# Operands of the last stage made from columns of x with factors by one-hot matmuls, in place of gathered rows that are multiplied and transposed

## The reference, cut to what matters

```
def _ln(x, g, b):
    m = jnp.mean(x, axis=-1, keepdims=True)
    v = jnp.mean((x - m) ** 2, axis=-1, keepdims=True)
    return (x - m) * jax.lax.rsqrt(v + EPS) * g + b
h = _ln(x, pw_g[pathway_ids], pw_b[pathway_ids])
h = _ln(h, cp_g[compartment_ids], cp_b[compartment_ids])
t = _ln(x, tm_g[time_steps], tm_b[time_steps])
s = _ln(x, ms_g[scale_type], ms_b[scale_type])
cat = jnp.concatenate([w[0]*h, w[1]*t, w[2]*m, w[3]*n, w[4]*r, w[5]*s], axis=-1)
u = _ln(silu(cat @ int_W1 + int_b1) @ int_W2 + int_b2, int_g, int_be)
q = clip(round(u / u_scale))      # by rows, to 255 levels
out = x + (q @ q_rhs) * u_scale * rhs_scale
```

## Time and profile before

| | us |
|---|---|
| median of 3 runs (lowest to highest) | 1751.22 (1750.68 to 1754.04) |
| the profiled execution | 1750.74 |
| its span | 1748.8 |
| PE busy | 1733.7 (99%) |
| DVE busy | 1192.6 (68%) |
| ACT busy | 878.1 (50%) |
| POOL busy | 786.8 (45%) |

### The profile page before, as it was taken

One profiled execution on the slowest core, in us unless ns is written; L12 is line 12 of the kernel. 1 busy time (PEld: TensorE's weight loads), 2 busy tenths in 40 slices (PEclk: granted clock), 3 DMA queues, 4 the chain that ended last, 5 costly groups with the idle time before them and its releaser, 6 DMA issues. The chain is left out here.

```text
span 1748.8 us, 23364 instructions
## 1 busy us (share of the span) xinstructions
PE 1733.7 (99%) x7935; PEld 1407.0 (80%) x7935; DVE 1192.6 (68%) x1756; ACT 878.1 (50%) x1301; POOL 786.8 (45%) x702
## 2 busy tenths in 40 slices
PE   9999999999999999999999999999999999999998
PEld 7888888888778888888888888778877787787786
DVE  8756667669989678786563335357886687587555
ACT  7655555565666565674562223243453443443433
POOL 1112221122766566665560000025577877878742
PEclk9999999999999999999999999999999999999999
DMA  6011110120233324222536568877645445544511
GB/s 208 1 49 49 48 39 9 49 73 25 97 132 119 134 97 168 97 97 85 187 139 222 193 197 281 325 254 245 217 132 183 143 159 175 155 159 152 170 38 61
DMA packets 121991, 234.36 MB, mean 134 GB/s; under 512 B 25618, under 2 KB 25874, under 8 KB 121892
## 3 DMA queue, kind: packets, MB, share of 16 engines
q1 hardware_dynamic: 91732, 157.63, 27.0%
q0 software_dynamic: 11776, 41.95, 7.0%
q10 hardware_dynamic: 18384, 33.56, 5.8%
HBM read 170.71 MB, written 58.72 MB: 131 GB/s over the span
## 5 line engine op out<-in xcount | busy, mean ns | idle before, releaser
L1070 PE MATMUL bank<-h_parts,mlp_w 128*128 128x512 f32 x2016 | 460.0, 389 | 4.6 <-DVE mlp_w L1493 3.3
L1070 PEld LDWEIGHTS bank<-h_parts,mlp_w 128*128 128x128 f32 x2016 | 378.0, 188 | 85.4 <-DVE mlp_w L1493 3.7
L353 PE MATMUL bank<-h_parts,gate_w 128*128 128x512 f32 x1536 | 351.1, 389 | 0.6 <-DVE h_parts L688 0.5
L353 PEld LDWEIGHTS bank<-h_parts,gate_w 128*128 128x128 f32 x1536 | 288.1, 188 | 61.9 <-issue 0.9
L2066 PE MATMUL bank<-operand_parts,int_w 128*128 128x512 f32 x1152 | 279.8, 396 | 0.5 <-DVE u_tiles L2716 0.4
L1135 PE MATMUL bank<-p_parts,mlp_out_w 128*128 128x512 f32 x1152 | 271.2, 393 | 0.0
L1135 PEld LDWEIGHTS bank<-p_parts,mlp_out_w 128*128 128x128 f32 x1152 | 213.8, 188 | 48.4 <-issue 4.2
L2066 PEld LDWEIGHTS bank<-operand_parts,int_w 128*128 128x128 f32 x1152 | 212.2, 188 | 47.1 <-issue 2.2
L615 POOL TENSOR_TENSOR decay_sq<-decay 128x512 f32<-128x512 f32 x32 | 39.3, 1227 | 278.8 <-DVE decay L701 278.8
L1408 POOL TENSOR_TENSOR product_out<-product_out,gelu 128x512 f32<-128x512 f32 x69 | 120.0, 1762 | 97.1 <-DVE product_out L1564 96.6
L1288 ACT ACTIVATE product_copy<-bank,vec_sb 128x512 f32<-128x512 f32 x144 | 99.1, 688 | 112.4 <-PE bank L1070 111.4
(11 more groups left out here) (311 smaller groups left out, 2760.4 us busy)
## 6 DMA issues: line engine op xcount, KB each, us to landing
p_tile<-p_d ACTq DMA_DIRECT2D x96, 256.0 KB, 4.8
p_d<-product_out SPq DMA_DIRECT2D x92, 256.0 KB, 2.0
raw_mlp_w<-mlp_gate_g SPq DMA_DIRECT2D x21, 512.0 KB, 3.7
raw_mlp_w<-mlp_fc_g SPq DMA_DIRECT2D x21, 512.0 KB, 4.4
xin<-xT SPq DMA_DIRECT2D x8, 1024.0 KB
hs_d<-u SPq DMA_DIRECT2D x8, 1024.0 KB, 5.0
hs_pair<-hs_d SPq DMA_DIRECT2D x8, 1024.0 KB, 7.5
x_columns<-xT SPq DMA_DIRECT2D x8, 1024.0 KB, 6.9
```

What stands on the lines that cost most here:

```text
L353: i = pe.matmul(bank[:], gw[:, w, s, k, m * P:(m + 1) * P], hr[:, q, t, k, :], start=k == 0 and n == 0, stop=k == KT - 1 and n == 2)
L1070: i = pe.matmul(bank[:], wb[g % 2][:, s, w, kk, :], hop[u % 2][o][:, t, kk, :], start=first and kk == 0 and n == 0, stop=kk == 1 and n == ...
```

## The change

**Time and scale operands.** x columns are normalised as columns. POOL makes, for each of the four column tiles k, two passes over 128x512 (`xhat_columns`): xn[k] = x column times 1/std, then plus shift, both along the tokens. The factors come from `spread`: SP stores `rstd` and `shift` to DRAM (`store_stats`; 16 bytes, the four tiles' values, a partition), and loads them back to all 128 partitions (`load_stats`, two loads of 2 KB a partition). In that row the tokens of one tile of 128 are 16 bytes apart, so `spread_of` reads it with a step of 16 bytes; x and xn are read and written in the order of tokens.

**Gains.** A table `gains` (made once: each gain's high part and the rest of it, in groups of 32 rows) is multiplied on PE by the one-hot code `oh`, with 32 rows: one matmul of 128x512 an item, in place of four transposes. The bank then holds the gain of each token and feature. DVE multiplies xn[k] by the bank (`gain_product`): for t into `tn` (two buffers), for s in place. The bank is free after that product; high and low part are made from SBUF operands.

**What is gone.** `gather_ts`, `scale_rows`, `t_product`, and the eight items of four transposes in a block that turn t and s.

**Order.** Items stand by a table: those for steps 8 to 11 before step 6, those for 12 to 15 before step 10, with the bias matmuls there too. DVE's products stand by a table of their own. POOL makes k = 0 and 1 of the next block between the two pairs of residual additions, k = 2 and 3 at the start of the next block. In block 0 POOL makes all four behind the MLP half, and `first_order` puts the first two and the second four items behind the step that follows them. ACT's centring of the next x rows waits for the products of h, no longer for those of t and s.

The diff, cut to its core:

```diff
     def add_items(s):
         o, k = steps[s]
-        items.append((FRONT[o], k, ("op_low", NS, s, 0)))
+        items.append((FRONT[o], k, {"h": ("op_low", NS, s, 0), "t": ("t_prod", KT, k, 0), "s": ("s_prod", KT, k, 0)}[o]))
...
     order = []
     for s in range(NS):
-        if s % 2 == 0 and XF <= s + AHEAD < NS:
-            for ahead in (AHEAD, AHEAD + 1):
-                add_items(s + ahead)
-                order.append(("item", len(items) - 1))
+        for later in ITEMS_AT.get(s, ()):
+            add_items(later)
+            order.append(("item", len(items) - 1))
...
-    for n in (0, 4):
-        at_main = next(i for i, x in enumerate(first_order) if x == ("item", n)) + 2
-        first_order.insert(at_main - 2, first_order.pop(at_main))
+    for n, count in ((0, 2), (4, 4)):
+        at_main = next(i for i, x in enumerate(first_order) if x == ("item", n)) + count
+        first_order.insert(at_main - count, first_order.pop(at_main))
...
+    def gain_of(kind, k):
+        group = (2 * k + (kind == "ts")) % 4
+        return slice(GROUP * group, GROUP * (group + 1)), k // 2
+
+    def source(b, s):
+        o, k = steps[s]
+        if o == "x":
+            return x_columns(b, k)
+        return {"h": lambda: bank("th", k)[:], "t": lambda: tn[:, k % 2], "s": lambda: xn[:, k]}[o]()
...
+        def store_stats(b):
+            sp.wait_ge(S["x_rs"], 2 * (b + 1))
+            for c, t in enumerate((rstd, shift)):
+                sp.dma_start(stats_d[c].rearrange("(n p t) -> p n t", p=P, t=TT)[:, bass.ds(b, 1), :], t[:, XS:XS + 1, :])                  .then_inc(stats_stored, 16)
+
+        def load_stats(b):
+            sp.wait_ge(stats_stored, 32 * (b + 1))
+            if b:
+                sp.wait_ge(xn_add, KT * b)
+            for c in range(2):
+                sp.dma_start(spread[:, c, :], stats_d[c:c + 1, bass.ts(b, BT)].partition_broadcast(P)).then_inc(stats_loaded, 16)
+
+        def tail(b, nxt, nxt2):
...
             residual(0)
             residual(1)
+            if nxt:
+                store_stats(b + 1)
             turn(0)
+            if nxt:
+                load_stats(b + 1)
             if nxt2:
                 sp.wait_ge(S["xh_done"], TT * (b + 2))
...
-    T_AT = 0
...
+    ITEMS_AT = {2: (4, 5), 4: (6, 7), 6: (8, 9, 10, 11), 10: (12, 13, 14, 15)}
+    GAINS_AT = {6: (8, 9), 7: (10, 11), 10: (12, 13), 11: (14, 15)}
+    BIAS_AT = 10
...
+            elif kind in ("tt", "ts"):
+                if isinstance(b, int) and b == 0:
+                    pe.wait_ge(gain_done, 1)
+                pe.wait_ge(S["oh_done"], b + 1)
+                group, c = gain_of(kind, k)
+                i = pe.matmul(dst[:], gains[group, c, :], oh[group, :], start=True, stop=True, tile_position=(group.start, 0))
...
+            if s == BIAS_AT:
+                if isinstance(b, int) and b == 0:
+                    pe.wait_ge(tab_done, 1)
+                pe.wait_ge(S["oh_done"], b + 1)
+                for m in range(KT):
+                    rows_m = slice(GROUP * m, GROUP * (m + 1))
+                    pe.matmul(A[m][:], bias_t[rows_m, :], oh[rows_m, :], start=False, stop=False, tile_position=(GROUP * m, 0))
...
-        def gather_ts(b, t, first):
-            if first:
-                pool.wait_ge(S["tt_ps"], KT * b)
-                pool.wait_ge(S["ts_ps"], KT * b)
-                pool.wait_ge(S["g_fence"], FENCES * b + TT + 2)
-                pool.tensor_tensor(fence[:, 3:4], mh4[:, 0:1], mh4[:, 0:1], ALU.mult).then_inc(S["g_fence"], 1)
-            pool.indirect_dma_start(gts[t][:].rearrange("p r d -> p (r d)"), None, ins["ts_rows"][:],
-                                    bass.IndirectOffsetOnAxis(ap=row_now[:, t:t + 1], axis=0)).then_inc(ts_rows, 16)
-
-        def scale_rows(b):
-            pool.wait_ge(S["xh_done"], TT * (b + 1))
-            pool.wait_ge(ts_rows, 16 * TT * (b + 1))
-            for t in range(TT):
-                pool.tensor_tensor(gts[t][:, 1], gts[t][:, 1], xh[:, t, :], ALU.mult).then_inc(S["s_prod"], 1)
+        def by_tile(columns):
+            return columns.rearrange("p (t q) -> p t q", t=TT)
+
+        def spread_of(c):
+            return spread[:, c, :].rearrange("p (q t) -> p t q", t=TT)
+
+        def xhat_columns(b, k):
+            first = isinstance(b, int) and b == 0
+            if not first:
+                pool.wait_ge(xs_loaded[k % 2], 16 * (2 * b + k // 2))
+                pool.wait_ge(S["op_low"], NS * (b - 1) + XF + KT + 2 * k + 2)
+            elif k < 2:
+                pool.wait_ge(xs_loaded[k], 16)
+            else:
+                pool.wait_ge(first_loaded, 32)
+            pool.wait_ge(stats_loaded, 32 * (b + 1))
+            pool.tensor_tensor(by_tile(xn[:, k]), by_tile(x_columns(b, k)), spread_of(0), ALU.mult).then_inc(xn_mul, 1)
+            pool.wait_ge(xn_mul, KT * b + k + 1)
+            pool.tensor_tensor(by_tile(xn[:, k]), by_tile(xn[:, k]), spread_of(1), ALU.add).then_inc(xn_add, 1)
...
-                scale_rows(b)
+                xhat_columns(b, 2)
+                xhat_columns(b, 3)
...
-                for t in range(TT):
-                    gather_ts(b + 1, t, t == 0)
+                xhat_columns(b + 1, 0)
+                xhat_columns(b + 1, 1)
...
-        def t_product(b, t):
-            dve.wait_ge(S["xh_done"], TT * b + t + 1)
-            dve.wait_ge(ts_rows, 16 * TT * (b + 1))
-            dve.tensor_tensor(gts[t][:, 0], gts[t][:, 0], xh[:, t, :], ALU.mult).then_inc(S["t_prod"], 1)
...
+        def gain_product(b, s):
+            o, k = steps[s]
+            dve.wait_ge(S[FRONT[o] + "_ps"], KT * b + k + 1)
+            dve.wait_ge(xn_add, KT * b + k + 1)
+            dve.tensor_tensor(source(b, s), xn[:, k], bank(FRONT[o], k)[:], ALU.mult).then_inc(S[o + "_prod"], 1)
...
-                if T_AT <= s < T_AT + TT:
-                    t_product(b, s - T_AT)
+                for later in GAINS_AT.get(s, ()):
+                    gain_product(b, later)
```

104 lines of the change are left out of this document (59 added, 45 removed).

## The result

The changed kernel takes 1794.2 us (median of 4 runs, 1791.82 to 1797.73) against 1752.6 for the kernel before (4 runs): the ratio is 1.0235, interval 1.0219 to 1.0252. It is 41.6 us slower; the forecast was 9 us faster, the range ended at 1762 and the slowest case at 1775. The profiled execution has a span of 1791.9 us. First the page of the changed kernel, busy times and granted clock, then PE's waits from 1200 us on.

A forecast was written before the change was run, and what follows sets the result against it. PE, busy 99%, was taken as the bound. A cut of 17.1 us, less 6 x 1.2 for meetings of DVE and POOL and 1.0 for block 0, gave -8.9: 1751.2 to 1742 us, range 1733 to 1762.

The forecast's parts named there:

- PE's part: Time and scale operands on PE: transposes of 3.48 us a block become eight matmuls of 1.34, saving 2.14 us.
- the sentence on the h factors: POOL's h factors come 23.3 us after the row work, so 46.3 us after the block's start, one earlier.
- Half a meeting: DVE operations meeting POOL passes around the second matmul group: 0.8 us of PE idle for hidden parts, 0.4 for u.
- the second rival: Give-back as large as the cut: DVE operations meet POOL passes, PE waits 2.1 us a block; 1748, chance 0.25.
- six further DVE products: In the cut-eaten case, six DVE products besides three hidden parts each meet a POOL pass, 1.1 us at a time.
- the first two rivals: First: cut kept whole, 1734, chance 0.15. Second: cut eaten by DVE meeting POOL's passes, 1748, chance 0.25.
- POOL's ring: POOL's work round one block: 48.7 us plus two times X for its passes, 60.9 us, under PE's new 61.9.
- The third rival: Slower: the step of 16 bytes makes a POOL pass 2.29 us, its ring 67.0; +15 us, 1766, chance 0.20.
- the low part of step 7: DVE operand PE needs before step 6: fits by some tenths, cost nothing; PE waits there if POOL is late.
- DMA: Spread loads ahead of x tiles and transposes in the queues: 0 to 1.7 us a block, costed at 0.
- Waits at the ff items: Sign of a wrong forecast: PE waits there, for transposes behind the spread loads, by more than 0.5 us a block.
- Block 0: First block of the last stage: items 6 and 7 wait for ACT to empty two banks, 1.0 us.

The follow-up runs named there:

- the run with products in PSUM: Changed kernel with DVE writing t and s products back into the gain's PSUM bank, held until the low part, items in pairs again: 1805.3 us.
- short loads: Changed kernel with the two statistics loads going to 4 partitions in place of 128 in blocks 1 to 7: 1789.2 us.
- late loads: Changed kernel with the two statistics loads issued behind the fourth transpose of a q tile in place of the first: 1791.9 us.
- the kernel before with half the transposes: Kernel before, two of four PE transposes of each t and s item left out in blocks 1 to 7: 1747.9 us.
- hidden values first on ACT: Changed kernel with hidden values 0 to 2 ahead of the centring of the first two h tiles on ACT: 1790.4 us.

## Why the prediction was wrong

**PE's part: right, and a little low.** From a block's start to `main_last` PE took 42.0 us before (1474.07 to 1516.10 in its timeline) and takes 39.4 now (1712.48 to 1751.87, no waits in either): 2.6 us saved, where 2.14 was taken and 2.60 was the upper bound. The changed kernel's chain:

```profile
1730.76 0.43 PE bank L2075 x2
1731.20 11.15 PE bank L2119 x48
1742.34 0.44 PE bank L2075 x4
1742.78 0.23 PE bank L2105 x3
```

Eight gain matmuls and the four bias ones take 1.10 us together, forecast 2.01.

**The step that failed is the sentence on the h factors.** The prediction let them come 46.3 us after the block's start, one earlier than read, because DVE's scales come earlier. They came at 51.1. (The 47.3 was taken from one block; over blocks 1 to 5 the kernel before has 48.2.) In the block from 1433.12 nothing came earlier: POOL's first row of h stands 24.1 us after the start, 24.2 before. From there to the h factors the prediction kept 23.3 us ("and so don't move against B"); they took 26.6. POOL's wait for the third gather is 1.3 us longer, the last two operations on rows of h 1.0, and an earlier one and the issues of two gathers 1.0. The last two items are the meetings with DVE's low parts of t and s, whose source had moved from PSUM to SBUF; the run with products in PSUM shows them. The prediction had counted the meetings with POOL's *new* passes, not those of DVE's new operands with POOL's old work: the move of the low parts' source was an edit with a cost, and it was given none. Why the gather lands later is open in the main: of the 9.0 us that POOL waits longer for gathered rows in six blocks, short loads took away 3.1 and late loads 3.9.

**The size of the meetings.** Half a meeting for the low hidden parts and half a one for u: 1.2 us a block. Measured: each of the four low hidden parts meets a pass and gets 1.2 us longer. For the hidden parts that is the second rival's mechanism, priced at 2.1 us a block with the "six further DVE products". These further ones cost nothing new: before, two low parts of x took 2.4 to 4.0 us and four products of h 2.5 to 4.7 at a block's end (blocks 1 to 5), beside the residual additions; now they take 3.5, and 2.5 to 3.9. From the h factors to the next block's start the chain takes 15.8 us with undisturbed parts (the kernel before with half the transposes) and 20.3 in the changed kernel (1483.85 to 1504.18). Of these 4.5 us 2.1 are the lower clock and the rest, by difference, the slow parts. The forecast had 16.8 there (64.0 - 2.1 + 1.2 = 63.1 for the block, less 46.3), so of the 8 us by which this block is longer than forecast 4.4 lie ahead of the h factors and 3.5 behind them.

**The slack.** The forecast and the first two rivals measured what is added against PE's length after the cut, and held the other rings to be shorter by a microsecond or more: POOL's ring, 48.7 + 2X, was summed with its waits as they were. The bound was not POOL's sum (by the windows it is busy 54 to 58 us of 70), but, by the rows, a chain over five engines, which nobody had added up; the run with less on PE shows it at 63.6. The account of the block from 1433.12 is then 63.6 + 2.9 (h factors at 50.7 in place of 47.8) + 2.4 (parts) + 2.1 (clock) = 71.0, and it took 71.1. This is the same chain read in two runs, and no test of it by itself. The first four of the six blocks take 70.7 to 71.2, the other two 69.7 and 67.4.

**The third rival** had the sign, with +15 us (1766) where +41.6 was measured, but not the mechanism. Its pass of 2.29 us is not there: undisturbed 1.53, as forecast (1.52), and 1.71 and 1.80 on the mean. PE never waits for the low part of step 7 in blocks 1 to 7.

**DMA.** Cost taken as 0, range 0 to 1.7 us a block: 10.2 us in all, 1.5 a block, near the range's far end. Waits at the ff items by more than 0.5 us a block were one of the signs that the prediction had named for being wrong. As a cause they are small: with the loads undone alone the median is 2 to 5 us lower, within what the intervals leave open.

**Block 0** was given 1.0 us. It is 9.5 longer: PE waits 3.45 us at the items of steps 12 to 15 for a bank that DVE's L3020 (`rhs_peak`, setup work) has still to read, 1.5 at step 4, and 12 matmuls behind the first of these waits (granted clock 0.54) take 5.29 us in place of 2.99, at the lower clock; the block's end has 3.9 us of waits.

**The lower clock** was in no case of the prediction. With PE at 99% nothing in the trace of before showed it.

## What to carry to other kernels

When the busiest engine is at 99%, find out what stands behind it before pricing a cut: take some work out of that engine in a run of its own and see how much comes back. Here 5 of 12 us did, and in a steady block half a microsecond (64.0 to 63.6). That run would have shown that a cut of 2 us a block had little to win and every new microsecond on the chain to lose.

A change that moves an operand from PSUM to SBUF is not neutral on DVE, even at the same 0.68 us: list the operations that get two SBUF operands and everything that POOL does beside them, its old work too. And what frees one operation from such a meeting can hand it to the next in the same queue: with hidden values first on ACT the waits at the hidden parts fell by 18 us and the time by 4.

## What was not expected of the hardware

- A POOL pass of 128x512 with one of two operands read at a step of 16 bytes takes 1.52 us against 1.26 to 1.28 dense, undisturbed: 1.2 times, less than the 1.5 that the figures of the Trainium skill (GPSIMD Engine Reference, "Performance pitfalls for Q7 kernels") make.
- DVE beside POOL: 0.69 us with a PSUM operand in all of 32 cases, 2.02 at the median with two SBUF operands. POOL feels it as well: rows of h 1.7 to 1.8 us in place of 1.3, and the issue of a gather 1.53 in place of 1.07 at the same place before. With DVE's products in PSUM both are back (rows of h 1.28, issues 1.06 on the mean).
- Two stores of 512 pieces of 4 bytes each hold their reader back by over 21 us; with 128 pieces of 16 bytes each it was 3.1, in the one block of six where the loads waited for them at all.
- After the waits of the second matmul group the granted clock fell in five of seven blocks (the 42 matmuls behind them took 10.6 to 12.4 us), and stayed up in two (9.78 us): after waits of 1.04 + 1.01 us and of 0.29 + 1.05 + 1.01 us. It fell after 1.12 + 1.05 + 0.35 us as well. What decides it was not looked into.
